# Turning delta through VectorE's 32x32 blocks and sixteen small DMAs in place of TensorE transposes, with the scores moved to follow the second projection

## The reference, cut

```python
def _L0_gnn_ref(h, adjacency, W_left, b_left, W_self, b_self, W_right, b_right, gamma, beta):
    u = einsum('bld,bmd->blm', h, h) / sqrt(d)
    delta = softmax(u, axis=-1) * adjacency
    attn = delta / (sum(delta, axis=2, keepdims=True) + 1e-10)
    h_left  = einsum('bld,ed->ble', h, W_left)  + b_left
    h_self  = einsum('bld,ed->ble', h, W_self)  + b_self
    h_right = einsum('bld,ed->ble', h, W_right) + b_right
    ctx = where(j > i, attn, 0) @ h_left + diag(attn)[..., None] * h_self + where(j < i, attn, 0) @ h_right
    o = (ctx - mean(ctx)) / sqrt(var(ctx) + 1e-12) * gamma + beta
    return relu(o)
x = layernorm(x + _L0_gnn_ref(x, adj, ...), axis=-1)
```

## Time and profile before

| | |
|---|---|
| median of 3 runs | 522.84 us (522.25 to 522.88) |
| the profiled execution, device time | 522.73 us |
| its span in the trace | 521.0 us |
| granted TensorE clock, mean | 0.987 |
| busy: PE, ACT, DVE, POOL | 96%, 63%, 61%, 45% |
| DMA, share of the 16 engines, all queues | 28.7% |

### The profile page before, as it was taken

The page is one execution under the profiler, slowest core; times in us unless marked ns, Lnnn a source line. Parts: engine busy times, 40 slices in busy tenths (PEclk is TensorE's granted clock), DMA queues, the critical chain, the costliest instruction groups (busy, mean ns, idle before and its releaser), DMA issues.

```text
span 521.0 us, 9473 instructions
## 1 busy us (share of the span) xinstructions
PE 498.4 (96%) x3030; PEld 487.6 (94%) x3030; DVE 315.4 (61%) x844; ACT 328.6 (63%) x740; POOL 236.7 (45%) x233
## 2 busy tenths in 40 slices
PE   6899999999999999999999999999999999999980
PEld 6799999999999999999999999999999999999980
DVE  2565666666565656566666556565656666656652
ACT  4655567576667676657667656757565766665642
POOL 0243345553345554344554334555334455433454
PEclk9899999999999999999999999999999999999996
DMA  8802332123333123333112333212333311330001
GB/s 261 274 0 83 112 111 92 52 81 113 111 111 109 36 77 111 111 111 111 66 70 85 111 111 111 103 42 77 111 111 111 111 52 71 100 111 32 31 30 60
DMA packets 40849, 49.11 MB, mean 94 GB/s; under 512 B 2176, under 2 KB 40832, under 8 KB 40832
## 3 DMA queue, kind: packets, MB, share of 16 engines
q1 hardware_dynamic: 40832, 48.90, 28.5%
HBM read 36.31 MB, written 12.58 MB: 94 GB/s over the span
## 4 chain that ended last, share of the span: by engine, by line
POOL 33%; issue 32%; PE 20%; ACT 5%; DVE 5%; DMA 2%; POOLq 1%; SPq 1%; ACTq 0%; DVEq 0%
PE ps_proj L271 12%; POOL scaled L628 11%; POOL shifted L632 9%; POOL dt_right L618 6%; POOL rstd L624 5%; PE ps_ctx L315 5%; ACT normed L391 3%; PE ps_scores L271 2%; POOL dt_left L618 2%; DMA w_raw<-in_L_gnn_W_right 2%; DVE proj_lo L475 1%; DVE shift L511 1%; DVE dt_full L480 1%; PE ps_dt L302 1%; ACT ps_proj L370 1%
## 5 line engine op out<-in xcount | busy, mean ns | idle before, releaser
L271 PE MATMUL ps_proj<-w_hi,xt_hi 128*128 128x384 f32 x576 | 197.0, 342 | 4.3 <-DVE w_lo L532 2.6
L271 PE MATMUL ps_proj<-w_hi,xt_lo 128*128 128x384 f32 x576 | 194.1, 337 | 0.0
L271 PE MATMUL ps_proj<-w_lo,xt_hi 128*128 128x384 f32 x576 | 194.1, 337 | 0.0
L370 ACT ACTIVATE ps_proj<-bias 128x384 f32<-128x384 f32 (+1 forms) x192 | 90.3, 498 | 80.3 <-DVE proj_lo L475 76.4
L624 POOL TENSOR_TENSOR rstd<-var_eps,minus_half 128x4 f32<-128x4 f32 x33 | 33.8, 1024 | 226.2 <-DVE var_eps L504 224.4
L271 PEld LDWEIGHTS ps_proj<-w_hi,xt_hi 128*128 128x128 f32 x576 | 108.6, 189 | 4.8 <-DVE w_lo L532 2.9
L271 PEld LDWEIGHTS ps_proj<-w_lo,xt_hi 128*128 128x128 f32 x576 | 108.6, 189 | 0.0
L271 PEld LDWEIGHTS ps_proj<-w_hi,xt_lo 128*128 128x128 f32 x576 | 108.6, 188 | 0.0
L374 ACT ACTIVATE proj_hi<-ps_proj 128x384 fp32r<-128x384 f32 x128 | 62.8, 491 | 58.5 <-PE ps_proj L271 58.5
L475 DVE TENSOR_TENSOR proj_lo<-ps_proj,proj_hi 128x384 fp32r<-128x384 f32 x128 | 70.7, 553 | 42.0 <-ACT proj_hi L374 38.4
L628 POOL TENSOR_TENSOR scaled<-normed,gamma_sb 128x384 f32<-128x384 f32 x64 | 76.1, 1189 | 34.3 <-ACT normed L391 31.4
(11 more groups left out here) (62 smaller groups left out, 732.8 us busy)
## 6 DMA issues: line engine op xcount, KB each, us to landing
xt_sb<-in_x_t SPq DMA_DIRECT2D x32, 384.0 KB, 3.5
x_sb<-in_x SPq DMA_DIRECT2D x32, 384.0 KB, 4.1
out_dram<-out_sb SPq DMA_DIRECT2D x32, 384.0 KB, 2.5
adj_sb<-in_adj SPq DMA_DIRECT2D x32, 256.0 KB, 4.2
w_raw<-in_L_gnn_W_left SPq DMA_DIRECT2D x1, 576.0 KB, 4.2
w_raw<-in_L_gnn_W_right SPq DMA_DIRECT2D x1, 576.0 KB, 8.4
w_raw<-in_L_gnn_W_self SPq DMA_DIRECT2D x1, 576.0 KB, 9.4
bias<-in_L_gnn_b_left SPq DMA_DIRECT2D x1, 192.0 KB, 5.1
```

The costliest lines, as they stand in the source:

```text
L271: mm = nc.tensor.matmul(to, stationary, moving, start=(k == 0 and not seeded), stop=(k == len(passes) - 1), skip_group_check=seeded)
L370: nc.scalar.activation(ps_proj[bank(at, g)][:, 0:to], bias[w][:, 0:to], ACT.Copy).then_inc(proj_seeded, 1)
```

## The change

Delta is turned in two steps that use neither PE nor PSUM. DVE's `transpose` works on 32x32 blocks, each within its own 32 partitions. It writes `turned`, in which block column q of every block lies together (128 words, 512 bytes a partition). SP then issues sixteen DMAs from SBUF to SBUF, one for each pair of a partition quarter a of `turned` and a quarter q of `dt_raw`, 32 partitions of 512 bytes each; each raises `dt_loaded` by 16. ACT and DVE make the high and the low part of `dt_full` from `dt_raw` once all sixteen have landed. The blocks of `dt_full` now stand in the order of (row tile, column tile), so that the diagonal ones are 0 and 3, and POOL cuts the triangles in four instructions of 256 elements where it had two of 512.

On PE the transposes are gone and `scores` of the next batch stands after the second projection. ACT and DVE orders are written anew around this, `xt_hi` and `xt_lo` are rings of four and split two batches ahead, `rstd` and `shift` are doubled, and at the start SP loads x_t of batch 1 ahead of the second weight.

```diff
@@ sync
+            def turn(at):
+                sp.wait_ge(turned_ready, at.n(1, 1))
+                for a in range(Q):
+                    for q in range(Q):
+                        sp.dma_start(dt_raw[q * R:(q + 1) * R, a, :, :].rearrange("p k r -> p (k r)"),
+                                     turned[a * R:(a + 1) * R, q * P:(q + 1) * P]).then_inc(dt_loaded, 16)
...
                     sp.dma_start(adj_sb[0][:], adj_rows[0]).then_inc(adj_loaded[0], 16)
+                    sp.dma_start(xt_sb[1][:], xt_rows[1]).then_inc(xt_loaded[1], 16)
...
                         load(ahead.n(1), ahead.slot(UNROLL))
+                if nxt.exists(BATCHES):
+                    turn(nxt)
+                if behind.exists(BATCHES):
                     store(behind)
@@ tensor
-                mm = nc.tensor.transpose(ps_dt[:, i, :], delta[:, t, m * P:(m + 1) * P], ident[:])
...
                 project(at, 0)
                 project(at, 1)
-                turn_delta(at)
-                project(at, 2)
...
                 if nxt.exists(BATCHES):
                     scores(nxt)
+                for g in range(2, NG):
+                    project(at, g)
@@ scalar
             def split_delta(at):
-                act.wait_ge(dt_ready, at.n(1, 1))
-                nc.scalar.activation(dt_full[:, 0, :, :], ps_dt[:], ACT.Copy).then_inc(dt_hi_ready, 1)
+                act.wait_ge(dt_loaded, at.n(256, 256))
+                nc.scalar.activation(dt_full[:, 0, :, :].rearrange("p k (a r) -> p k a r", a=Q),
+                                     dt_raw[:].rearrange("p a k r -> p k a r"), ACT.Copy).then_inc(dt_hi_ready, 1)
@@ vector
+            def turn(at):
+                dve.wait_ge(delta_ready, at.n(1, 1))
+                if at.b != 0:
+                    dve.wait_ge(dt_loaded, at.n(256, 0))
+                nc.vector.transpose(turned[:].rearrange("p (q k r) -> p k q r", q=Q, k=T * T),
+                                    delta[:].rearrange("p t (h q c) -> p (t h) q c", q=Q, c=R)).then_inc(turned_ready, 1)
@@ gpsimd
-                for to, sign in ((dt_left, 1), (dt_right, -1)):
+                for t in range(T):
+                    for to, sign in ((dt_left, 1), (dt_right, -1)):
```

More of the change, by code:

```diff
@@ L131, in gnn_resnorm @@
         on_diag = sb("on_diag", [P, T, P])
+        turned = sb("turned", [P, Q * T * T * R])
+        dt_raw = sb("dt_raw", [P, Q, T * T, R])
         dt_full = sb("dt_full", [P, 2, T * T, P], F32R)
@@ L146, in gnn_resnorm @@
         var_eps = sb("var_eps", [P, 2 * T])
-        rstd = sb("rstd", [P, 2 * T])
-        shift = sb("shift", [P, 2 * T])
+        rstd = [sb(f"rstd{i}", [P, 2 * T]) for i in range(2)]
+        shift = [sb(f"shift{i}", [P, 2 * T]) for i in range(2)]
         normed = sb("normed", [P, T, H])
@@ L239, in _ @@
                     sp.dma_start(adj_sb[0][:], adj_rows[0]).then_inc(adj_loaded[0], 16)
+                    sp.dma_start(xt_sb[1][:], xt_rows[1]).then_inc(xt_loaded[1], 16)
             for to, vector in ((gamma_sb, gamma), (beta_sb, beta)):
                 sp.dma_start(to[:], vector.partition_broadcast(P)).then_inc(vectors_loaded, 16)
-            sp.dma_start(x_sb[0][:], x_rows[0]).then_inc(x_loaded[0], 16)
-            for b in range(1, UNROLL):
+            sp.dma_start(adj_sb[1][:], adj_rows[1]).then_inc(adj_loaded[1], 16)
+            for b in range(2):
+                sp.dma_start(x_sb[b][:], x_rows[b]).then_inc(x_loaded[b], 16)
+            turn(Batch(0, 0))
+            for b in range(2, UNROLL):
                 load(b, b)
@@ L250, in one @@
             def one(at):
-                ahead, behind = at.plus(2), at.plus(-2)
+                ahead, behind, nxt = at.plus(2), at.plus(-2), at.plus(1)
                 if behind.exists(BATCHES):
@@ L390, in normalise @@
                 for t in range(T):
-                    nc.scalar.activation(normed[:, t, :], ps_ctx[:, t, 0:H], ACT.Identity, bias=shift[:, t:t + 1],
-                                         scale=rstd[:, t:t + 1]).then_inc(normed_ready, 1)
+                    nc.scalar.activation(normed[:, t, :], ps_ctx[:, t, 0:H], ACT.Identity, bias=shift[at.slot(2)][:, t:t + 1],
+                                         scale=rstd[at.slot(2)][:, t:t + 1]).then_inc(normed_ready, 1)
             def outputs(at):
+                nxt = at.plus(1).slot(2)
                 act.wait_ge(shift_ready, at.n(1, 2))
@@ L416, in _ @@
             exps(first)
+            split_xt(first.plus(1))
             def one(at):
                 nxt = at.plus(1)
-                before, second = at.plus(-1), at.plus(-2)
+                before, second, ahead = at.plus(-1), at.plus(-2), at.plus(2)
                 split_proj(at, 0)
+                split_delta(at)
                 if before.exists(BATCHES):
@@ L437, in one @@
                     seed_proj(nxt, 1)
-                    seed_proj(nxt, 2)
+                if ahead.exists(BATCHES):
+                    split_xt(ahead)
                 seed_ctx(at, 1)
                 if nxt.exists(BATCHES):
+                    seed_proj(nxt, 2)
+                if second.exists(BATCHES):
+                    outputs(second)
+                if nxt.exists(BATCHES):
                     seed_proj(nxt, 3)
-                    exps(nxt)
             every_batch(act, BATCHES, one)
@@ L479, in split_delta @@
                 dve.wait_ge(dt_hi_ready, at.n(1, 1))
-                nc.vector.tensor_tensor(dt_full[:, 1, :, :], ps_dt[:], dt_full[:, 0, :, :].bitcast(F32),
+                lo, hi = (dt_full[:, half, :, :].rearrange("p k (a r) -> p k a r", a=Q) for half in (1, 0))
+                nc.vector.tensor_tensor(lo, dt_raw[:].rearrange("p a k r -> p k a r"), hi.bitcast(F32),
                                         ALU.subtract).then_inc(dt_lo_ready, 1)
@@ L549, in _ @@
             deltas(first)
+            turn(first)
             dve.wait_ge(ident_ready, 1)
+            diagonal(first)
+            split_xt(first.plus(1))
             def one(at):
                 before, second = at.plus(-1), at.plus(-2)
-                nxt = at.plus(1)
+                nxt, ahead = at.plus(1), at.plus(2)
                 if before.exists(BATCHES):
@@ L573, in one @@
                     residual_stats(before, 1)
+                if ahead.exists(BATCHES):
+                    split_xt(ahead)
+                if before.exists(BATCHES):
                     dve.wait_ge(stats2_ready, before.n(T, T))
-                split_proj(at, 3)
+                context_stats(at, 0)
                 if before.exists(BATCHES):
                     residual_moments(before)
[L578 to L582, removed]
             every_batch(dve, BATCHES, one)
```

71 lines of the change are left out of this document (33 added, 38 removed).

## The result

| | before | after |
|---|---|---|
| median device time | 522.55 us (4 runs, 522.24 to 522.88) | 618.7 us (4 runs, 617.89 to 619.76) |
| ratio to before, 95% interval | | 1.184 (1.183 to 1.186) |
| span of the profiled execution | 521.0 | 618.0 |
| time of one batch in the middle | 15.42 | 18.02 |
| first projection of batch 1 | 30.52 | 41.11 |

The kernel is 18.4% slower. The forecast was 508 us with a range of 504 to 532. The page shows at once that PE no longer sets the time.

What follows compares the result with a forecast made beforehand. PE, busy 96% of the span, was taken as the bound. Batch 1's start at 38.3, 30 batches of 14.67 and an end of 27.6 gave a 506.0 us span; with 1.73 to device time, 508 us, range 504 to 532.

Steps and rivals of the forecast that it cites:

- The loop: New cycle from one `neg_max` to the next through every engine but POOL and PE: 14.50 us per batch.
- the slower rival: Sixteen small transfers one behind the other, paced by SP or queue: 16.0 us per batch, 549 us; chance of slower 0.29.
- the fifteen issues: SP's further DMA issues after the first of sixteen: 0.43 us each, 6.45 in all, bounds 6.15 to 7.95.
- `dt_full` to the next delta: ACT and DVE work after the DMAs: 3.32 us to `neg_max`, then 1.28 to delta.
- the second way: From `dt_full` over `normed`, POOL's two and the residual to delta: 4.4 against 4.6 us; a blocked POOL adds to it.
- The decision point: Cycle length at which the new time passes the old: 15.15 us, or 0.47 per issue at a landing of 1.8.
- the spare 0.17 us: Room per batch between the 14.50 us cycle of delta and PE's 14.67 us of products.
- the landing: Last small DMA's issue to its arrival: 1.8 us, the middle of 1.1 to 2.5.
- PE's floor of 14.67 us: PE's products alone per batch: 15.42 less 0.75 us, reached only if the next batch's delta is back in time.
- the stall of the seed: PE's wait for ACT's seed before the context: 0.30 us a batch, expected to go.
- that of the transposes: PE's four transposes turning delta: 0.45 us a batch, expected to go.
- The start: Batch 1 begins at 38.3 us against 30.5, since batch 0 waits for its small DMAs: 7.8 us lost.

Runs made afterwards that it cites:

- The first probe: Kernel before plus nine groups of eight DMAs behind its last store; a group took 4.94 to 5.04 us with SBUF on both sides, 3.59 to 3.68 with DRAM on one.
- The run with delta first: Changed kernel with DVE's delta and block transpose of the next batch moved ahead of the first half of the residual: 601.8 us, ratio 1.154.
- the run with twelve DMAs: Changed kernel without the four DMAs of equal quarters, so part of the attention is left out: 538.5 us, ratio 1.031 to the kernel before.

## Why the prediction was wrong

The loop was the right mechanism, and the slower rival named it: the pace at which small DMAs can be issued. The size of one term, the fifteen issues, was off, and that decided the sign.

| term of the loop | predicted | measured |
|---|---|---|
| delta to the block transpose | 0.81 | 0.80 |
| the block transpose, to SP's first issue | 0.69 + 0.10 | 0.74 |
| fifteen issues | 15 x 0.43 = 6.45 | 15 x 0.628 = 9.42 |
| last issue to ACT's `dt_full` | 1.8 + 0.05 | 1.79 |
| `dt_full` to the next delta | 3.32 + 1.28 = 4.60 | 5.27 |
| sum | 14.50 | 18.02 |

- **The issues, 2.97 of the 3.52 us.** This is the step that failed: the term was put at 15 x 0.43 = 6.45 us and took 9.42. I took 0.43 from three loads and reasoned that the time of an issue grows with its rows, so that 32 rows would come out near the low end. The first probe shows that rows (16 to 128) and bytes play no part in it and the memories do. All three loads had DRAM on one side, and no row of the trace had an SBUF to SBUF DMA at all. The three rows had spoken against the reasoning: the shortest issue, 0.37, is `x_t` with 384 rows, and the two longer ones have 256 each, so that both have eight times the 32, and the one with twelve times was the quick one. My upper end of 0.53 was the largest gap in those rows, not a bound for another kind of transfer. Even with all high ends the predicted loop was 17.4 us, and 18.02 lies over it.
- **The way to the next delta, 0.67.** I had found the second way, over `normed`, POOL and the residual, and put it at 4.4 against 4.6 us. It took 5.27, so the loop did go through POOL, which mine left out. `y_sb` lasted 1.35 us instead of 0.56 while POOL ran `scaled` beside it, and delta stood behind it on DVE. The run with delta first gave 0.61 of it back. What the Trainium skill says of the port that two such instructions share ("SBUF — State Buffer", § Who interferes with whom: DVE with two inputs in SBUF contends with a POOL instruction that reads SBUF) agrees with these rows. The other half of the residual in the same batch, with POOL idle, kept its 0.56:

```profile
221.16 0.56 DVE L545 SCALAR_TENSOR_TENSOR y_sb<-shifted,x_sb 128x384 f32<-128x384 f32 x1
```

- **The decision point.** The prediction put it at 0.47 us per issue. The loop without its issues took 18.02 - 9.42 = 8.60 us and not 8.05, and in the run with twelve DMAs as well (15.50 less eleven steps of 0.63 are 8.6). By that the point lies at (15.15 - 8.60) / 15 = 0.44, hardly above the forecast's own 0.43. Issues at 0.43 would have made a loop of 15.05 us and, by the prediction's formula, some 520 us and not 508. Both are estimates from these runs, but they say that the spare 0.17 us was not there.
- **The block transpose (0.71 against 0.69) and the landing (1.76 against 1.8)** were right, though both had wide bounds; the landing was the middle of a range and so partly luck.
- **PE's floor of 14.67 us** was right to within 0.02, as three runs under it with periods of 14.69 show. That the stall of the seed went was right; its share and that of the transposes, 0.30 and 0.45, come out at 0.21 and 0.52.
- **The start.** Batch 1 began at 41.11 and not 38.3: the sixteen of batch 0 landed at 31.03 and not 28.2, which is the same dear issues, 15 x 0.2 us.
- **The sum.** Turned delta to turned delta, from batch 0 to batch 31, takes 18.11 us on average, a little over the 18.02 of the middle, since some batches have single issues that last longer (one of 1.32 us in the batch of 19.12 us that begins at 71.69). The prediction's own formula, 508 + 31 x (loop - 14.67), gives 615 us for it, and with the 2.8 us of the later start 617, against 618.7 measured. PE's granted clock fell from a mean of 0.987 to 0.943, but that did not lengthen the batches. In the first stretch below it was 0.91 and delta to delta took 17.94 us, in the second it was 1.00 and they took 18.04 (columns as above):

```profile
91.00:109.00 18.00, 15.75 (x88) 15.46 (x87) 10.87 (x28) 10.09 (x23) 6.81 (x10) 0.91 0.32 96
109.00:127.00 18.00, 16.05 (x97) 15.41 (x96) 10.68 (x28) 10.09 (x23) 6.69 (x10) 1.00 0.32 96
```

## What to carry to other kernels

Count DMA issues like instructions when they stand on a loop: number times price, on one engine, and the landing of the last one on top. Take their price from a transfer of the same kind, with the same memories on both sides; if the trace has none, measure eight of them in an empty stretch before building on them. When a shuffle between partitions needs many small SBUF to SBUF DMAs, one store to DRAM and a few loads that carry the permutation on the DRAM side can be the shorter way: here 5.4 us against 11.2.

## What the runs showed of the hardware

- An issue with SBUF on both sides costs 0.63 us of the issuing engine (0.59 and a gap of 0.04), one with DRAM on either side 0.46, back to back. The first is the same for 16 to 128 partitions and 8 to 64 KB, the second for loads of 32 partitions (16 KB) and 128 (64 KB).
- SP and ACT issue independently: 4.99 and 5.33 us for eight each at the same time.
- A 16 KB DMA lands 1.8 us after its issue SBUF to SBUF, 1.7 from DRAM and 1.5 to DRAM.
- VectorE turned 128x512 float32 in 32x32 blocks in 0.71 us, where its product of the same size (`delta`) took 0.67.
- `y_sb`, a VectorE instruction on two SBUF operands, took 1.35 us beside POOL's `scaled` and 0.56 with POOL idle.
